# Graph layer and ternary feed-forward on one core: output blocks turned in the degrees' bank, six product banks and six turned rows in the table stage

## What is computed

```python
# graph layer, x = layernorm(input)
deg = segment_sum(ones_like(src), dst, N)
agg = segment_sum(x[src], dst, N)
h = x @ W_self + b_self + (agg / maximum(deg, 1)[:, None]) @ W_neigh
h = layernorm(h) * gamma + beta
h = where(h >= 0, h, alpha * h)
x1 = input + h + x
# feed-forward layer, on layernorm(x1); the weights are quantised to -s, 0, s in groups of 128 inputs
hid = silu(ln @ wq_gate.T) * (ln @ wq_up.T)      # 512 -> 1408
out = x1 + hid @ wq_down.T                       # 1408 -> 512
```

## Time and profile before

| | kernel before |
|---|---|
| median of 3 runs | 1559.13 us (1558.26 to 1559.78) |
| the profiled execution, its own time | 1556.55 us |
| span of that execution in the profile | 1554.8 us |
| PE busy | 1483.5 us, 95% |
| DVE busy | 1074.3 us, 69% |
| ACT busy | 1141.7 us, 73% |
| POOL busy | 947.8 us, 61% |
| matmuls of the steps (L931 + L932, up and down) | 416.1 + 415.6 + 208.2 + 208.1 us |
| gather sums (L846 + L848) | 323.2 + 321.1 us |
| chain that ended last | PE 74%, DVE 10%, issue 4%, POOL 4%, ACT 4%, DMA 3% |

### The profile page before, as it was taken

One profiled execution on the slowest core, in us unless ns is written; L12 is line 12 of the kernel. 1 busy time (PEld: TensorE's weight loads), 2 busy tenths in 40 slices (PEclk: granted clock), 3 DMA queues, 4 the chain that ended last, 5 costly groups with the idle time before them and its releaser, 6 DMA issues.

```text
span 1554.8 us, 21492 instructions
## 1 busy us (share of the span) xinstructions
PE 1483.5 (95%) x6421; PEld 764.6 (49%) x6422; DVE 1074.3 (69%) x2336; ACT 1141.7 (73%) x1986; POOL 947.8 (61%) x936
## 2 busy tenths in 40 slices
PE   6889998999998999999999999999999999999997
PEld 3434444454654555555555455555555545554443
DVE  7899963565767476675766756757666666675975
ACT  3434430102988979899797888988989989999886
POOL 2211217776777777777777777777777777773000
PEclk9999999999999999999999999999999999999999
DMA  8967639899888888998888888888888878884100
GB/s 299 261 183 247 190 109 335 297 307 323 247 265 224 251 248 254 256 238 241 242 251 252 229 242 221 270 245 242 244 227 249 239 227 237 229 258 125 35 21 33
DMA packets 210384, 353.37 MB, mean 227 GB/s; under 512 B 104986, under 2 KB 104986, under 8 KB 210258
## 3 DMA queue, kind: packets, MB, share of 16 engines
q0 software_dynamic: 70560, 231.27, 52.0%
q1 hardware_dynamic: 139708, 120.73, 26.0%
HBM read 295.79 MB, written 39.62 MB: 216 GB/s over the span
## 4 chain that ended last, share of the span: by engine, by line
PE 74%; DVE 10%; issue 4%; POOL 4%; ACT 4%; DMA 3%; SPq 0%; DVEq 0%; ACTq 0%; POOLq 0%
PE f_ps L931 19%; PE f_ps L932 19%; PE f_ps L772 14%; PE agg_ps L846 10%; PE agg_ps L848 10%; POOL rows L724 4%; ACT f_ps L1008 2%; DMA xnt_rows<-work 2%; PE f_ps L876 1%; DVE st6p L1084 1%; DVE work L1340 1%; DVE hsx L1190 1%; DVE scl L1184 1%; DVE acc L1359 1%; DVE hsx L1189 1%
## 5 line engine op out<-in xcount | busy, mean ns | idle before, releaser
L724 POOL DMA_INDIRECT rows<-node_table,idx x882 | 896.6, 1017 | 302.5 <-issue 275.7
L1008 ACT ACTIVATE f_ps<-f_ps,ratio 128x512 f32<-128x512 f32 (+2 forms) x1303 | 775.0, 677 | 113.5 <-PE f_ps L932 107.2
L931 PE MATMUL f_ps<-x1T,tern 128*128 128x512 f16 (+2 forms) x1144 | 416.1, 368 | 21.5 <-DVE work L1340 13.5
L932 PE MATMUL f_ps<-x1T,tern 128*128 128x512 f16 (+2 forms) x1144 | 415.6, 367 | 0.0
L846 PE MATMUL agg_ps<-rows,hot 128*128 128x512 f16 x846 | 323.2, 382 | 4.6 <-DMA rows<-node_table,idx 3.6
L848 PE MATMUL agg_ps<-rows,hot 128*128 128x512 f16 x846 | 321.1, 380 | 0.0
L1359 DVE SCALAR_TENSOR_TENSOR acc<-f_ps,scl,acc 128x512 f32<-128x512 f32 (+2 forms) x143 | 102.2, 715 | 192.9 <-PE f_ps L932 125.7
L931 PE MATMUL f_ps<-hT,tern 128*128 128x512 f16 (+2 forms) x572 | 208.2, 367 | 3.2 <-DVE work L1340 2.8
L932 PE MATMUL f_ps<-hT,tern 128*128 128x512 f16 (+2 forms) x572 | 208.1, 367 | 0.0
L931 PEld LDWEIGHTS f_ps<-x1T,tern 128*128 128x128 f16 x1144 | 112.1, 98 | 135.9 <-DVE work L1340 21.2
L846 PEld LDWEIGHTS agg_ps<-rows,hot 128*128 128x128 f16 x846 | 119.5, 141 | 113.8 <-issue 31.5
(11 more groups left out here) (165 smaller groups left out, 1624.7 us busy)
## 6 DMA issues: line engine op xcount, KB each, us to landing
rows<-node_table,idx POOLq DMA_INDIRECT x882, 4.7
hsx<-own_rows SPq DMA_DIRECT2D x49, 256.0 KB, 3.9
hsx<-in_x SPq DMA_DIRECT2D x48, 256.0 KB, 5.1
out_nodes<-work SPq DMA_DIRECT2D x48, 256.0 KB, 4.0
node_table<-work SPq DMA_DIRECT2D x30, 256.0 KB, 3.3
xnt_rows<-work SPq DMA_DIRECT2D x26, 256.0 KB, 5.9
xj<-xnt_rows SPq DMA_DIRECT2D x26, 256.0 KB, 4.9
acc<-own_rows SPq DMA_DIRECT2D x23, 256.0 KB, 5.7
```

Source lines behind the costliest of these rows:

```text
L724: pool.indirect_dma_start(out=rows[:, j, :], out_offset=None, in_=table[:, :], in_offset=bass.IndirectOffsetOnAxis(ap=of[:, j:j + 1], axis ...
L931: pe.matmul(to, lhs, parts[0], start=g == 0, stop=False, skip_group_check=True)
L932: pe.matmul(to, lhs, parts[1], start=False, stop=True, skip_group_check=True).then_inc(p_ff, 1)
L1008: act.activation(ps, ps, ACT.Copy, scale=ratio[:, w if up else 2, j:j + 1]).then_inc(a_scaled, 1)
```

## The change

The output blocks of chunks 0 to 11 leave the lanes. Each is turned into the bank that held only the degrees (`deg_ps`, now `side_ps`) at a fixed tick: 11 or 16 of a slot up to 48, and 2, 6, 10 or 14 of a later one, at the first free place of a later tick than the fourth step behind the chunk's last down step (`TURN_AT`). DVE adds and SP stores it three ticks later (`ADD_TICK`). The turning waits for the adding of the block before it and for the reciprocal of the slot's degrees, and the degrees wait for the adding of the last block turned. The planner places only the four output blocks of the last chunk in lanes; NSTEPS becomes 1804 and SLOTS 56. Of the last chunk, two of the four final down groups are scaled by DVE and no longer by ACT.

In the table stage the products go round all six lanes (YB = 6), the ring of turned rows has six tiles (the three new ones in the unused part of `rows`), and product 0 is issued ahead of `turn0(1)`. POOL waits for the last product and for the stores of the ring before it gathers. PE's waits for the last high and low parts stand ahead of the overflow flag's branch, no longer behind it.

The diff, with context cut:

```diff
@@ -98,7 +98,6 @@
     AT = {}
-    OUT_FROM, OUT_EVERY = 0.1, 0.45
     PACE, EVEN = 38.0, 35.0
@@ -110,12 +109,11 @@
                 in_bank[bank_of] = None
-                if held_sums and held_sums[1] == "down" and held_sums[2:] == (1, 1):
-                    outs_left += [(pos + OUT_FROM + OUT_EVERY * j if held_sums[0] < CHUNKS - 1 else 0, FIRST[held_sums[0]] + j)
-                                  for j in range(SIZE[held_sums[0]])]
+                if held_sums == (CHUNKS - 1, "down", 1, 1):
+                    outs_left += range(FIRST[-1], BLOCKS)
                 own_at = max(own_left[0] - 0.75, own_free[NTH_LATER[own_left[0]]]) if own_left else 2 * BLOCKS
-                if outs_left and (outs_left[0][0] <= pos or not sums_left):
-                    b = outs_left.pop(0)[1]
+                if outs_left:
+                    b = outs_left.pop(0)
                     job = (CHUNK_OF[b], "out", b, 0)
@@ -194,14 +192,23 @@
+    TURN_AT, ADD_TICK = {}, {}
+    room = [(t, k) for t in range(BLOCKS + 8) for k in ((11, 16) if t < BLOCKS else (2, 6, 10, 14))]
+    for c in range(CHUNKS - 1):
+        for j in range(SIZE[c]):
+            while room[0] <= AT_OF[LAST_DOWN[c] + 4]:
+                room.pop(0)
+            t, k = room.pop(0)
+            TURN_AT[t, k] = FIRST[c] + j
+            ADD_TICK[t + (k + 3) // TICKS, (k + 3) % TICKS] = FIRST[c] + j
+            assert (t, k) < min((FIRST[c] + j + X1R, 9), *(AT_OF[SID[c + 1, "down", 0, FT - 1, w]] for w in range(2)))
     OUT_SID = {i: s for s, (c, kind, i, g, w, bank_of) in enumerate(FSTEPS) if kind == "out"}
-    assert list(OUT_SID) == list(range(BLOCKS))
+    assert list(OUT_SID) == list(range(FIRST[-1], BLOCKS))
     ADD_AT = {}
     for b, s in OUT_SID.items():
-        c = CHUNK_OF[b]
-        assert s > LAST_DOWN[c] and (c == CHUNKS - 1 or s < min(SID[c + 1, "down", 0, FT - 1, w] for w in range(2)))
+        assert s > LAST_DOWN[-1]
         ADD_AT.setdefault(min(s + 3, NSTEPS - 1), []).append(b)
-        assert AT_OF[s] < (b + X1R, 9)
     SLOTS = max(AT)[0] + 1
@@ -331,8 +338,8 @@
         ystage = [work16[:, i] for i in range(3)] + [hsxflat[:, i * D:(i + 2) * D] for i in (8, 10)]
-        XTR = 3
-        xnT_ring = [work[:, 3 + i].rearrange("p (k n) -> p k n", k=KT) for i in range(XTR)]
+        XTR = 6
+        xnT_ring = [tile.rearrange("p (k n) -> p k n", k=KT) for i in range(3) for tile in (work[:, 3 + i], rows32[:, 15 + i])]
         held = [x1Tflat.bitcast(F32)[:, i * D:(i + 1) * D].rearrange("p (k n) -> p k n", k=KT) for i in range(HELD_X)]
@@ -348,9 +355,9 @@
         hit = [tern32[0:EP, w, 0:BLOCKS * NSEG].rearrange("p (b s) -> p b s", b=BLOCKS) for w in (1, 2)]
-        YB = 4
+        YB = LANES
         own_ps = f_ps[LANES - 1]
-        t_ps, y_ps = [agg_ps, deg_ps], f_ps
+        t_ps, y_ps = [agg_ps, side_ps], f_ps
@@ -408,7 +415,7 @@
         def out_bank(b):
-            return f_ps[FSTEPS[OUT_SID[b]][5]]
+            return f_ps[FSTEPS[OUT_SID[b]][5]] if b in OUT_SID else side_ps
@@ -672,6 +679,8 @@
                         load_own(t + 2)
+                    if (t, k) in ADD_TICK:
+                        store_out(ADD_TICK[t, k])
             for b in range(BLOCKS - 4, BLOCKS):
@@ -716,8 +725,11 @@
             pool.wait_ge(a_xn, BLOCKS)
+            pool.wait_ge(p_y, BLOCKS)
             for i in range(YR):
                 pool.wait_ge(st_y[i], 16 * len(range(i, BLOCKS, YR)))
+            for i in range(XTR):
+                pool.wait_ge(st_xt[i], 16 * len(range(i, len(LATER), XTR)))
@@ -774,7 +786,7 @@
             for i in range(BLOCKS):
-                if i + 1 < BLOCKS:
+                if 0 < i < BLOCKS - 1:
                     turn0(i + 1)
@@ -784,6 +796,8 @@
                 mm.then_inc(p_y, 1)
+                if i == 0:
+                    turn0(1)
@@ -823,6 +837,8 @@
             pe.wait_ge(a_xnT, BLOCKS)
+            pe.wait_ge(a_yhi, BLOCKS)
+            pe.wait_ge(v_ylo, BLOCKS)
             for i in range(WTR):
@@ -831,7 +847,9 @@
                 after(pe, v_inv, b)
-                pe.matmul(deg_ps[:, 0:1], degs[:, :], ones[:, 0:1], start=True, stop=True).then_inc(p_deg, 1)
+                after(pe, v_out, turned_back[0])
+                pe.matmul(side_ps[:, 0:1], degs[:, :], ones[:, 0:1], start=True, stop=True).then_inc(p_deg, 1)
@@ -868,13 +886,23 @@
-            def turn_out(b):
+            turned_back = [0]
+            def turn_out(b, degrees):
                 c = CHUNK_OF[b]
                 t = b - FIRST[c]
-                pe.wait_ge(a_dn, KT * (c + 1))
+                if c < CHUNKS - 1:
+                    pe.wait_ge(a_dn, KT * (c + 1))
+                    after(pe, v_out, b)
+                    pe.wait_ge(v_inv, degrees)
+                    turned_back[0] = b + 1
+                else:
+                    pe.wait_ge(a_dn, KT * c + 2)
+                    pe.wait_ge(v_dn, 2)
                 for k in range(KT):
                     mm = pe.transpose(out_bank(b)[:, k * P:(k + 1) * P], yT[:, k, t * P:(t + 1) * P], identf[:, :])
-                mm.then_inc(p_ff, 1)
+                mm.then_inc(p_t4 if c < CHUNKS - 1 else p_ff, 1)
@@ -905,13 +933,15 @@
                     elif pkind == "down":
-                        pe.wait_ge(a_dn, DN_NTH[pc, pi, pw])
+                        if kind != "out":
+                            pe.wait_ge(a_dn, DN_NTH[pc, pi, pw])
                     elif pw == 0:
...
                 if kind == "out":
-                    turn_out(i)
+                    turn_out(i, BLOCKS)
                     return
@@ -931,9 +961,6 @@
-            pe.wait_ge(a_yhi, BLOCKS)
-            pe.wait_ge(v_ylo, BLOCKS)
             pe.wait_ge(v_scl, 1)
@@ -946,6 +973,8 @@
                         degree(t)
+                    if (t, k) in TURN_AT:
+                        turn_out(TURN_AT[t, k], min(t + 1, BLOCKS))
                     if t < BLOCKS:
@@ -1016,11 +1045,10 @@
                     act.activation(acc[:, 0, u % 2, 0:width], ps, ACT.Silu, scale=scl[:, 0, j:j + 1]).then_inc(a_silu, 1)
-                elif kind == "down":
+                elif kind == "down" and not (c == CHUNKS - 1 and w):
                     act.wait_ge(p_ff, s + 1)
-                    if c:
-                        act.wait_ge(p_ff, OUT_SID[FIRST[c] - 1] + 1)
+                    after(act, p_t4, FIRST[c])
                     act.activation(yT[:, 2 * i + w, 0:width], ps, ACT.Copy, scale=scl[:, 2, j:j + 1]).then_inc(a_dn, 1)
@@ -1317,7 +1345,7 @@
                 chain_done()
-                chain(dve.tensor_scalar(inv[:, 2:3], deg_ps[:, 0:1], 1.0, osc[:, 0:1], ALU.max, ALU.mult))
+                chain(dve.tensor_scalar(inv[:, 2:3], side_ps[:, 0:1], 1.0, osc[:, 0:1], ALU.max, ALU.mult))
                 chain_done()
@@ -1335,7 +1363,10 @@
                 i, n = nth_out(b)
-                dve.wait_ge(p_ff, OUT_SID[b] + 1)
+                if b in OUT_SID:
+                    dve.wait_ge(p_ff, OUT_SID[b] + 1)
+                else:
+                    dve.wait_ge(p_t4, b + 1)
                 after(dve, st_out[i], 16 * n)
@@ -1358,6 +1389,11 @@
                                              in1=acc[:, 0, u % 2, 0:width], op0=ALU.mult, op1=ALU.mult).then_inc(v_h, 1)
+                elif kind == "down" and c == CHUNKS - 1 and w:
+                    dve.wait_ge(p_ff, s + 1)
+                    dve.wait_ge(p_t4, FIRST[c])
+                    dve.tensor_scalar(yT[:, 2 * i + w, 0:width], ps, scl[:, 2, j:j + 1], None, ALU.mult).then_inc(v_dn, 1)
                 if (kind, g) == ("own", KT - 1):
@@ -1474,6 +1510,8 @@
                         low_x1(t - 2)
+                    if (t, k) in ADD_TICK:
+                        add_out(ADD_TICK[t, k])
                     next(part, None)
```

More of the change, by code:

```diff
@@ L310, in build @@
         dstv_o = sb("dstv_o", [P, STEPS], F32)
-        agg_ps, deg_ps = bank("agg_ps"), bank("deg_ps")
+        agg_ps, side_ps = bank("agg_ps"), bank("side_ps")
         f_ps = [bank(f"f_ps{i}") for i in range(LANES)]
@@ L397, in build @@
                              "v_own"))
-        p_used, p_deg, p_sd, p_own, p_ff = (
-            sem(n) for n in ("p_used", "p_deg", "p_sd", "p_own", "p_ff"))
+        p_used, p_deg, p_sd, p_own, p_ff, p_t4 = (
+            sem(n) for n in ("p_used", "p_deg", "p_sd", "p_own", "p_ff", "p_t4"))
         a_xx, a_neg, a_x1s, a_hi1, a_scaled, a_silu, a_hi, a_dn = (
             sem(n) for n in ("a_xx", "a_neg", "a_x1s", "a_hi1", "a_scaled", "a_silu", "a_hi", "a_dn"))
-        v_scaled, v_h, v_hlo, v_out = (sem(n) for n in ("v_scaled", "v_h", "v_hlo", "v_out"))
+        v_scaled, v_h, v_hlo, v_out, v_dn = (sem(n) for n in ("v_scaled", "v_h", "v_hlo", "v_out", "v_dn"))
         o_ld, o_hot, o_rows, o_used, o_agg, o_hs, o_sum, o_st, o_dl, o_inv = (
```

## The result

The changed kernel takes 1565.22 us, the median of 16 runs (1559.48 to 1570.97), beside 1559.35 us (1556.62 to 1563.11) for the kernel before: ratio 1.0033, 95% interval 1.0021 to 1.0045. I had forecast 2.4 us faster; it is some 5 us slower. The profiled execution spans 1563.6 us where that of before spans 1554.8. Every ratio in this document is of runs measured side by side and comes with its own interval; it is not the quotient of the two medians and can differ from that by 0.001. One execution of the kernel before, beside the last four experiments, took 5050.41 us and is in no ratio.

The account below looks back on a forecast made before the run. TensorE was taken to bound the main loop (911.6 of 923 us busy), VectorE the stretches to 232 and from 1428 to 1467 us. Terms -1.4 -13.7 +4.7 +1.3 +7.1 +0.6 -0.5 -0.5 gave -2.4: 1556.7 us, range 1546 to 1566.

Parts of the forecast that it names:

- table stage: Up to the first gather: six banks and six turned rows save 1.4 us (bounds -3 and +1).
- lanes' waits for L1340 before 1428, and half clock: Main loop: eleven PE waits for DVE's output adding and a half-clock stretch go, -13.7 us (at least -10.5).
- turnings' waits before slot 49: Side bank: tick 11 turnings wait for the reciprocal, +4.7 us, tick 16 turnings for the adding, +1.3.
- x1T at chunks 9 to 12: Earlier chunk starts make PE wait for x1T: 5.7 us at chunk 10, 0.6 at chunks 9 and 11.
- half clock behind these: PE at half clock after chunk 10's x1T wait in slot 42: +1.4 us.
- behind slot 48, without x1T: To 1467 us DVE sets the pace, so removing PE's waits moves little: -0.5 us (-7 to +3).
- last evictions: Kernel's end: with two of ACT's four on DVE, the last ends earlier, -0.5 us (-0.7 to 0).
- The reciprocal: Nineteen tick 11 turnings wait for DVE's reciprocal, 0.25 us a slot: +4.7 us (0 to 31).
- the slower rival that hung on it: The nineteen tick 11 turnings wait 0.8 us each for the reciprocal: 1567.2 us, chance 0.12.
- The hole is covered: Slot 42: PE hardly waits for x1T at chunk 10, as ACT and DVE catch up: 1549.0 us, chance 0.28.
- The side bank's waits equal the lanes': Side bank waits cost 13.7 us in place of 6.0, so 1564.4 us; chance 0.08.
- The clock: Side bank waits drop PE's clock each time, eight of sixteen late ones at 1.4 us: 1567.9 us, chance 0.05.

Follow-up runs that it names:

- whole: The changed kernel as it is, measured again beside the kernel before: 1562.94 us, ratio 1.0045.
- table_only_b: The kernel before with only the table stage's part of the change: 1558.66 us, ratio 0.9998; table_only, its first run beside the 1722.11 us kernel before: 1.0009.
- whole_edges: The changed kernel, pace 38, with SP's load of the edge lists at tick 12 in place of 3: 1554.92 us, 0.9986 of before.
- before_39_b: The kernel before, outputs still in lanes, with the planner's pace at 39 steps a slot, not 38: 1571.85 us, ratio 1.0090.
- pace_37_b: The changed kernel with the planner's pace at 37 steps a slot, not 38: 1548.66 us, 0.9937 of the kernel before.
- tail_banks: The changed kernel with every second output turning from slot 49 on in the gather sums' bank: 1561.94 us, 1.0016 of the kernel before.
- edges_tail: The changed kernel at pace 37, edge-list load at tick 12, outputs from slot 49 on alternating between two banks: 1540.66 us, 0.9879 of before.
- the first four experiments: Beside a 1722.11 us kernel before: table part alone 1.0009, change without table part 0.9947, change at pace 37 0.9996, kernel before at pace 39 1.0039.

## Why the prediction was wrong, step by step

What happened is the forecast's own mechanism for the loss, the early chunk starts, at twice the size, and with it the sign. The time, 1565.22 us, lies inside the range that I gave (1546 to 1566); the direction is what was wrong. The terms, as far as the account gives them (whole against before):

| term | forecast | shown |
|---|---|---|
| table stage | -1.4 | 0 (table_only_b 0.9998) |
| lanes' waits for L1340 before 1428, and half clock | -13.7 | -13.1 (nine waits, 11.7, and 1.4), all gone |
| turnings' waits before slot 49 | +6.0 | +1.0 |
| x1T at chunks 9 to 12 | +6.3 | +13.3 |
| half clock behind these | +1.4 | +4.6 (2.9 at chunk 10, 1.7 at chunk 11) |
| behind slot 48, without x1T | -0.5 | 0 (waits +1.0, half clock -1.4, small gaps +0.4) |
| last evictions | -0.5 | -0.5 |

I had counted eleven lane waits before 1428, 10.5 us; the rows of before have nine, 10.2 us (the others of the fifteen come later), a miss of 0.6 us in the term. The turnings' waits, priced 5 us too dear, hid part of the larger miss; that was luck.

**The step that failed** is the sum for x1T. I had put chunk 10 at 5.7 and chunks 9 and 11 together at 0.6, and for chunk 12 I took that x1T would be ready. The waits are 7.8, 0.5, 3.3 and 1.6 in whole, 13.3 in sum.
- Of chunk 10, the handshakes were right: SP's second issue ends 7.7 us after PE is at tick 7 (I had 1.5 + 6.45 = 7.95), and PE's work from there is 5.3 (I had 5.2). What was wrong is the landing: 5.5 us from the end of the issue to PE's start where I took 3, between rows of 4.9 and 1.9. The row of 1.9 is from a slot without gathers. The row of 4.9, from a slot with them, gives 7.7; I had written the reason myself ("in a busy DMA") and then gone to the middle. But one row isn't the answer either: where chunk 10 waits, the landing took from 2.8 us (whole_edges, with a wait of 5.1) to 5.5 in the kernels' profiles, and at the other chunk starts under gathers up to 8.2. The 7.7 was the end of my own range for this wait.
- For chunks 9 and 11 I had compared PE's work behind tick 9 with chunk 2's, and for chunk 12 its work with that of before; for none had I made chunk 10's sum. Made for chunk 11 (in whole), there are 10.1 us of work behind tick 7, SP's issue ends 8.5 us behind it, and x1T lands 5.0 us later, at 13.4: 3.3 of wait.
- The half clock behind the longest wait lasted 5.4 us of PE's work, not 3.04 as behind a wait of 2.74 us, and there was a second stretch behind chunk 11's. I had priced the clock's stretch as if it had one length and came once.

The rows of chunk 11 in whole (PE at tick 7, SP's transposes, PE's first step of the chunk):

```profile
1375.13 0.38 PE L961 MATMUL f_ps<-x1T,tern 128*128 128x512 f16 x1
...
1379.80 3.79 SPq L608 DMA_TRANSPOSE x1T<-hsx  x2
...
1388.57 0.38 PE L961 MATMUL f_ps<-x1T,tern 128*128 128x512 f16 x1 [3.34 <-DMA x1T<-hsx]
```

That it isn't the side bank is shown by before_39_b, that it is the cost by pace_37_b.

**The reciprocal.** Nineteen turnings at tick 11 were to wait 0.25 us each. Six turnings start right behind the reciprocal, and the longest waits are 0.4 and 0.24 us, here the second:

```profile
1262.49 0.17 DVE L1350 RECIPROCAL inv<-inv 128x1 f32<-128x1 f32 x1
...
1262.81 0.41 PE L904 MATMUL side_ps<-identf,yT 128*128 128x128 f32 x2 [0.24 <-DVE inv L1350]
```

The turning stands behind tick 11's steps on PE; it comes 0.86 us after the tick's first matmul, and I had measured the lateness against that first matmul. So the term falls to some 1 us, and the slower rival that hung on it never came near. Its reasoning was half right: read as I had read the kernel before, the reciprocal is late in 20 of the 44 slots by 19.6 us in sum, where before it was 13 and 10.9. PE had other work to do meanwhile. The addings before slot 49 held up no turning.

**Behind slot 48** I had said that DVE sets the pace, so that the lanes' 7.0 us of waits would not be won, and that turnings four ticks apart bring back as much. Both hold: the lanes' waits went, 6.4 us of turnings' waits and 1.6 more of other waits came, and taking those away again (tail_banks, edges_tail) brought little.

**The table stage.** PE and ACT run ahead as said, and POOL's two tiles are 14.9 us apart, where they were 14.2:

```profile
198.27 1.15 POOL L714 TENSOR_TENSOR hsx<-hsx 128x512 f16<-128x512 f16 x1 [1.63 <-DVE hsx L1218]
...
213.17 2.26 POOL L714 TENSOR_TENSOR hsx<-hsx 128x512 f16<-128x512 f16 x2 [7.11 <-issue]
...
231.55 1.30 POOL L736 DMA_INDIRECT rows<-node_table,idx  x1 [13.74 <-issue]
```

The first gather came near 231.3, as said; but with the old table stage it came between 230.9 and 232.8 in four profiles and with the new one between 230.6 and 232.6 in ten, so the forecast's 1.4 is no more than two executions of one kernel differ by.

**The last evictions** were right: PE starts its last turnings after 0.91 us of idle time, not 1.44.

```profile
1552.92 1.94 PE L904 MATMUL f_ps<-identf,yT 128*128 128x128 f32 x16 [0.91 <-DVE yT L1396]
```

**The rivals.** "The hole is covered" (1549.0) is refuted by the row of chunk 10. "The side bank's waits equal the lanes'" is wrong by the account, 7.4 against 18.7. The clock didn't fall and rise with each short wait: none of the turnings' waits before slot 49 has half clock behind it, and neither have three in slot 49 of 1.2 to 2.5 us (clock 1.00 from 1428 to 1467). In the changed kernel's main loop the clock fell at single long waits, of 3 us and more, at 258, 504, 606, 1289 and 1391 us. In the kernel before it also fell at one of 2.58 us, at 1444, and in whole it didn't at one of 2.77, at 258. The Trainium skill's rule of frequent short idles ("TensorE: Matmul & The Clock Gate", section "A second HAM failure mode") named the pattern, but it isn't what these traces show.

## What to carry to other kernels

When an item leaves a hand-made plan, its positions leave too, and everything behind it starts earlier: check each point where a stage begins against the time its input lands, counting work ahead of it on the waiting engine, and give the positions back (here one in 38 turned +0.45% into -0.6%). Take a transfer's landing time from rows with the same traffic, and several of them, for it scatters (here 2.8 to 5.5 us at one place). And look at what stands ahead of a critical transfer on its queue: a load that was needed 12 ticks later held it up, and moving it was worth 0.5 to 0.6% in every version. All told, pace 37 with that load behind the turning gives 1542.02 us, 0.9888 of the kernel before (0.9870 to 0.9907), and better than the change as made.

## What the runs showed of the hardware that I had not expected

Beside the first four experiments, the very kernel that takes 1559 us beside all others took 1722. In table_only's profile PE's matmuls start 0.215 us apart as always, but ACT begins a scaling long after its matmul, while idle. PE's waits, and one such place (the scaling at 703.64 belongs to the matmul at 700.52):

```profile
PE f_ps L938 <- ACT f_ps L1013: 39.1, 45, 3.5
PE f_ps L938 <- issue: 36.6, 36, 3.5
PE f_ps L938 <- DVE work L1345: 31.0, 20, 4.8
```

```profile
700.52 0.38 PE L939 MATMUL f_ps<-x1T,tern 128*128 128x512 f16 x1
...
703.64 0.66 ACT L1013 ACTIVATE f_ps<-f_ps,ratio 128x512 f32<-128x512 f32 x1 [2.18 <-PE f_ps L775]
```

Of the 231 scalings ahead of which ACT was idle, 134 began over 1 us after their matmul's start; in the kernel before, of 154 none did (0.42 us in the median). At that place DVE and POOL resume late too, at 707.89 and 708.17, after 3.25 and 2.31 us of idle time. It looks as if PE's signals reached the others late; why, the profile doesn't show, and it stays open. The record has these four experiments on another chip (numbered 1) than the later ones (7, 11 and 13, at 1558 to 1560 us for the kernel before), so it may be that chip; nothing was run to tell. It does show that a ranking of kernels holds for the condition in which it was measured: there the outputs' part was a gain of 0.5%, and pace 37 worth nothing.
